# Moving work between steps of a two-recurrence pipeline: a 512-column split ahead of the candidate, routing one step earlier, two products into another PSUM bank

## What is computed

```
# LSTM, one step of 128
a = x_t @ Wx + h @ Wh + b;  i, f, o = sigmoid(...);  g = tanh(...)
c = f * c + i * g;  h = o * tanh(c)
# attention over the latents of h, then x = x + attn @ Wout
# GRU on the new x, one step of 128
z, r = sigmoid([x_t, h] @ Wz + bz), sigmoid([x_t, h] @ Wr + br)
cand = tanh([x_t, r * h] @ Wh + bh);  h = (1 - z) * h + z * cand
h_next = tanh(h @ Wp + bp) on every fourth step
# experts on the GRU's outputs: gate, top 2 of 8, gelu(x @ w1 + b1) @ w2 + b2, weighted sum, + x
```

## Time and profile before

| | |
|---|---|
| median of the runs | 589.99 us |
| the profiled execution | 591.56 us, its span 589.7 us |
| PE, DVE, ACT busy | 525.5, 424.1, 352.9 us |
| steps 74 to 81, one period of 8 | 31.01 us |
| PE busy in that period | 28.76 us |
| mean granted TensorE clock | 0.93 of 2.4 GHz |

### The profile page before, as it was taken

How to read it: one execution, slowest core, us unless ns; L and a number is a source line. 1 busy time by engine, 2 the same in 40 slices (tenths; PEclk the granted TensorE clock), 3 DMA queues, 4 the chain that set the end, 5 groups by cost and what they waited for, 6 DMA issues and landing times.

```text
span 589.7 us, 20148 instructions
## 1 busy us (share of the span) xinstructions
PE 525.5 (89%) x7315; PEld 483.4 (82%) x7356; DVE 424.1 (72%) x2402; ACT 352.9 (60%) x1297; POOL 33.6 (6%) x85
## 2 busy tenths in 40 slices
PE   7967887889789898989999989898999998889998
PEld 3736675888679898989888989898989988879998
DVE  4447678767776887878787878787879788664432
ACT  2235345775256676757676767676676767565562
POOL 6000000000000000000000000000000000000000
PEclk9679659699759999999999999999999999999999
DMA  8810101010100101010101010101101010100000
GB/s 204 327 15 6 20 1 20 3 13 10 16 11 6 16 5 17 12 20 3 19 12 17 7 15 16 12 10 12 16 14 13 4 17 13 18 1 3 11 7 10
DMA packets 75118, 14.32 MB, mean 24 GB/s; under 512 B 71411, under 2 KB 74111, under 8 KB 74638
## 3 DMA queue, kind: packets, MB, share of 16 engines
q1 hardware_dynamic: 74566, 11.96, 11.2%
q10 hardware_dynamic: 456, 1.08, 0.6%
HBM read 7.78 MB, written 1.05 MB: 15 GB/s over the span
## 4 chain that ended last, share of the span: by engine, by line
PE 68%; DVE 17%; issue 6%; ACT 6%; DMA 1%; SPq 1%; POOL 0%; DVEq 0%; ACTq 0%; POOLq 0%
PE pH L488 16%; PE pG L488 12%; PE pV L488 12%; PE pY L488 9%; PE pL L488 8%; PE pC L578 5%; PE pS L488 5%; ACT hid L864 2%; PE pC L488 2%; DVE latNlo L976 2%; DVE acc L1073 1%; DVE gB L1137 1%; DVE ghi L1140 1%; DVE glo L1143 1%; ACT gC L879 1%
## 5 line engine op out<-in xcount | busy, mean ns | idle before, releaser
L864 ACT ACTIVATE hid<-pH,b 128x256 f32<-128x256 f32 (+1 forms) x320 | 116.3, 433 | 3.9 <-PE pH L488 3.9
L488 PE MATMUL pY<-w,hid 128*128 128x128 f32 x608 | 85.1, 284 | 0.0
L488 PE MATMUL pH<-ghi,w1hi 128*128 128x256 f16 (+1 forms) x320 | 76.7, 254 | 9.1 <-ACT hid L864 7.3
L488 PE MATMUL pH<-ghi,w1lo 128*128 128x256 f16 (+1 forms) x320 | 77.0, 255 | 0.0
L488 PE MATMUL pH<-glo,w1hi 128*128 128x256 f16 (+1 forms) x320 | 76.9, 255 | 0.0
L488 PEld LDWEIGHTS pY<-w,hid 128*128 128x128 f32 x608 | 74.6, 193 | 0.2
L871 ACT ACTIVATE gT<-pG 128x32 f32<-128x32 f32 x128 | 24.7, 193 | 70.5 <-PE pG L488 70.3
L488 PE MATMUL pV<-w,hid 128*128 128x128 f32 x416 | 58.2, 283 | 0.0
L1124 DVE SCALAR_TENSOR_TENSOR gRZ<-gT,g 128x32 f32<-128x32 f32 x128 | 24.5, 191 | 46.6 <-ACT gT L871 46.0
L1137 DVE TENSOR_TENSOR gB<-gRZ,gC 128x16 f32<-128x16 f32 x128 | 22.5, 175 | 46.9 <-ACT gC L879 44.5
L879 ACT ACTIVATE gC<-pG 128x16 f32<-128x16 f32 x128 | 23.5, 183 | 52.9 <-PE pG L488 52.8
(11 more groups left out here) (177 smaller groups left out, 1569.6 us busy)
## 6 DMA issues: line engine op xcount, KB each, us to landing
w<-in_w SPq DMA_DIRECT2D x2, 2048.0 KB, 13.1
qbd<-qh SPq DMA_DIRECT2D x256, 16.0 KB, 1.9
out<-acc SPq DMA_DIRECT2D x16, 64.0 KB, 1.5
xT<-in_xT ACTq DMA_DIRECT2D x1, 960.0 KB, 8.2
hid<-in_WqT SPq DMA_DIRECT2D x1, 512.0 KB, 5.6
hid<-in_Wout SPq DMA_DIRECT2D x1, 512.0 KB, 10.3
lWh<-in_lWh SPq DMA_DIRECT2D x1, 256.0 KB, 2.8
lWx<-in_lWx SPq DMA_DIRECT2D x1, 256.0 KB, 3.1
```

Source lines behind the costliest of these rows:

```text
L488: return nc.tensor.matmul(o, lhsT=lhsT, rhs=rhs, start=start, stop=stop, skip_group_check=True)
L864: A(hid[:, e % NHID, c, 0:W], pH[half][:, W * at:W * (at + 1)], ACT.Gelu, bias=b1[:, e, c:c + 1], scale=1.0 / SP).then_inc(gelu, 1)
```

## The change

It reorders the loops and changes few operations.

- PTlo moves on DVE (k >= 18) from behind the cell to ahead of the wait for gC. mx moves ahead of slot B's combine. The cell is one block (rs now behind it), and latT and the rest of qh move from the start of the step into `between`, behind OT.
- Routing: `route_x` moves to the end of phase 1, its copies go to ACT at the end of that step (lg with a factor 0.5), route_first to phase 2; the subtraction `low` goes away, since tanh takes the negated maximum as its bias. latNhi and latNlo move to phases 2 and 3.
- Slot A of phases 2 and 3 goes to bank pC. Slot B's product of phase 6 goes to phase 0 (in pY).
- On ACT (k >= 18) the setup splits stand behind gT; the exp table is loaded behind gT of phase 3 and no more at the end of phase 2. The rest of qh is one DVE instruction in place of four.

```diff
-             (37, "B", 3, 0), (38, "B", 3, 1), (42, "A", 4, 0), ...
-             (44, "A", 6, 0), (44, "B", 6, 1), (45, "B", 7, 0), (46, "B", 7, 1))
+             (37, "B", 3, 0), (40, "B", 3, 1), (42, "A", 4, 0), ...
+             (44, "A", 6, 0), (44, "B", 6, 1), (45, "B", 7, 0), (48, "B", 7, 1))
 def route_stages(i):
-    at = GS * i + (26 if i < NG - 1 else 25)
-    if i > 12:
-        return at, at + 1, at + 2, at + 3, at + 3
-    return at, at + 1, at + 2, at + 6, at + 8
+    at = GS * i + 25
+    return (at, at + 1, at + 2, at + 3, at + 3) if i > 12 else (at, at + 1, at + 3, at + 7, at + 9)
+def down_bank(k, slot):
+    return "Y" if slot == "B" else "C" if k % TB in (2, 3) and k < LAST else "V"
-TO_EXP = [TB + O_S] + [k + 1 for k, half in UPS if half == 0 and (k + 1, 0) not in UPS and k < T]
+TO_EXP = [TB + O_S] + [k + 2 for k, half in UPS if half == 0 and (k + 1, 0) not in UPS and k < T]
 # turn_probs, then experts_down, on PE
+                if downs_before(k, "C"):
+                    pe.wait_ge(acc_done, downs_before(k, "C"))
+                        elif bank == "C":
+                            pe.wait_ge(q_lo, count(latents_at, k))
 # ACT, behind gT of the step
+                if k >= LAG:
+                    setup(k)
+                if k in TO_EXP:
+                    A(spare[:, 1:2], still[:, 0:1], ACT.Exp)
 # ACT, at the end of the step
-                setup(k)
+                if k < LAG:
+                    setup(k)
-                    A(th[:, n % 2, :], low[:, n % 2, :], ACT.Tanh, scale=0.5).then_inc(r_th, 1)
+                    A(th[:, n % 2, :], lg[:, n % 2, :], ACT.Tanh, bias=lmax[:, n % 2, 0:1]).then_inc(r_th, 1)
+                if k in ROUTES:
+                    route_copy(ROUTES[k])
 # DVE, between(k)
-                if unit_at(k, O_T) is not None:
+                if unit_at(k, O_T) is not None and k < LAG:
                     pt_rest(unit_at(k, O_T))
...
+                if latents_at(k) is not None:
+                    lat_copy(latents_at(k))
+                if latents_at(k - 1) is not None:
+                    q_rest(latents_at(k - 1))
...
-                if k % TB == 1 and TB < k <= T + 1:
+                if k % TB == 2 and TB < k <= T + 2:
                     turn_latents(k // TB - 1, lathi, latNhi)
 # DVE, the loop
+                if unit_at(k - 1, O_S) is not None:
+                    maximum(unit_at(k - 1, O_S))
                 if (k - 1, "B") in DOWN_AT:
                     combine(k - 1, "B")
+                if unit_at(k, O_T) is not None and k >= LAG:
+                    pt_rest(unit_at(k, O_T))
                 if k in PICK:
                     route_pick(PICK[k])
```

More of the change, by code:

```diff
@@ L117, in gelus_of, with downs_before @@
     return max(n for (vm, ve, h), n in GELUS.items() if (vm, ve) == (m, e))
-def downs_before(k, slot):
-    return max([ORDER[d] + 1 for (at, sl), ds in DOWN_AT.items() if sl == slot and at < k for d in ds], default=0)
+def downs_before(k, bank):
+    return max([ORDER[d] + 1 for (at, slot), ds in DOWN_AT.items() if down_bank(at, slot) == bank and at < k for d in ds], default=0)
 def count(at, upto):
@@ L374, in seq, with bank_of @@
             return t[:, :].rearrange("p (t b) -> p t b", b=B)[:, TB * p:TB * (p + 1), :].rearrange("p t b -> p b t")
-        def bank_of(slot):
-            return pV if slot == "A" else pY
+        def bank_of(k, slot):
+            return {"Y": pY, "C": pC, "V": pV}[down_bank(k, slot)]
         def keys(p):
@@ L405, in spread_queries @@
                 if u == 0:
[L406 removed]
+                    sp.wait_ge(q_lo, p + 1)
                 if n == 0:
@@ L829, in setup, with route_copy @@
                     A(gp, h0T[:, :], ACT.Copy).then_inc(g_p, 1)
+            def route_copy(n):
+                m, tg = visit_of(n)
+                act.wait_ge(r_mm, n + 1)
+                if n >= 2:
+                    act.wait_ge(r_ranked, n - 1)
+                A(lg[:, n % 2, :], pV[:, 256:256 + E], ACT.Copy, scale=0.5).then_inc(r_copy, 1)
+                if slots_used(m, tg):
+                    act.wait_ge(stored[2 * (m % 3) + tg], 16 * slots_used(m, tg))
+                A(acc[:, m % 3, tg, :], pV[:, 384:512], ACT.Copy).then_inc(r_copy, 1)
             def q_copy(p):
@@ L964, in q_rest @@
                 dve.wait_ge(q_hi, p + 1)
[L965 to L968, removed]
+                V.scalar_tensor_tensor(qh[:, p % 2, :, 1, :, :],
+                                       pC[:, :].rearrange("p (g s b) -> p b g s", g=HG, b=B), 1.0 / SP,
+                                       qh[:, p % 2, :, 0, :, :], ALU.mult, ALU.subtract).then_inc(q_lo, 1)
             def turn_latents(p, whole_t, turned):
@@ L1107, in setup_late, with cell, hidden @@
                     V.scalar_tensor_tensor(w1lo[:, e, :], w1[:, e, :], SW, w1hi[:, e, :], ALU.mult, ALU.subtract).then_inc(set_w1, 1)
-            def after_latents(k):
-                setup_late(k)
-                if latents_at(k) is not None:
-                    lat_copy(latents_at(k))
-                if latents_at(k - 1) is not None:
-                    q_rest(latents_at(k - 1))
-                if period_at(k) is not None:
-                    add_x(period_at(k))
+            def cell(t):
+                dve.wait_ge(l_tanh, t + 1)
+                V.scalar_tensor_tensor(lP[:, :, :], lT[:, 0:2, :], 1.0, lT[:, 3:5, :], ALU.add, ALU.mult).then_inc(l_mul, 1)
+                V.tensor_scalar(oK[:, :], lT[:, 2, :], SH / 2, SH / 2, ALU.mult, ALU.add)
+                dve.wait_ge(l_mul, t + 1)
+                V.scalar_tensor_tensor(lT[:, 4, :], lP[:, 1, :], 0.5, lP[:, 0, :], ALU.mult, ALU.add).then_inc(l_c, 1)
+            def hidden(t):
+                dve.wait_ge(l_tc, t + 1)
+                V.tensor_tensor(hhi[:, t + 1, :], oK[:, :], lC[:, :], ALU.mult).then_inc(l_hi, 1)
+                V.tensor_tensor(hfull[:, :], oK[:, :], lC[:, :], ALU.mult).then_inc(l_h, 1)
+                dve.wait_ge(l_h, t + 1)
+                V.tensor_tensor(hlo[:, t + 1, :], hfull[:, :], hhi[:, t + 1, :], ALU.subtract).then_inc(l_lo, 1)
             for k in range(STEPS):
@@ L1126, in _ @@
                     V.scalar_tensor_tensor(gA[:, :], gT[:, 1, :], -1.0, prev, ALU.add, ALU.mult).then_inc(g_a, 1)
+                if unit_at(k - 1, O_S) is not None:
+                    maximum(unit_at(k - 1, O_S))
+                if t < LAG:
+                    cell(t)
                 if (k - 1, "B") in DOWN_AT:
                     combine(k - 1, "B")
+                if period_at(k) is not None:
+                    add_x(period_at(k))
                 if k >= LAG:
-                    after_latents(k)
-                if unit_at(k - 1, O_S) is not None:
-                    maximum(unit_at(k - 1, O_S))
+                    setup_late(k)
+                if unit_at(k, O_T) is not None and k >= LAG:
+                    pt_rest(unit_at(k, O_T))
                 if k in PICK:
```

80 lines of the change are left out of this document (27 added, 53 removed).

## The result

The changed kernel takes 621.87 us (median of 4 runs, 621.58 to 623.97) against 590.0 (588.25 to 590.3): ratio 1.0554, 95% interval 1.0523 to 1.0585. The forecast was slower, 611 us, range 586 to 632. The profiled execution has a span of 620.0 us, 30.3 more than before.

What follows compares the result with a forecast made beforehand. PE was taken as near its limit, with DVE late in phases 2 to 5. Phase terms summed to +1.9, taken as +2.0 per period; ten periods plus outside steps gave +21, so 611 us, range 586 to 632.

Steps and rivals of the forecast that it cites:

- Phase 6, +0.55: Step 78: early PTlo delays gB, lC, table load and next gT; the product leaving gains nothing; +0.55 us per period.
- Phase 7, +0.05: Step 79: PTlo waits for PThi and holds gB, yet the state reaches PE in time; +0.05 us per period.
- Phase 0, +2.5: Step 80: moved product 1.0, PE's wait for latT 1.25, late start 0.76; +2.5 us per period.
- Phase 1, +0.3: Step 81: PE gets route_x, and the queries' spreading DMAs still end about when PE reaches the scores; +0.3 us per period.
- Phases 2 to 5, -1.5: Steps 74 to 77: PE loses route_x and waits for DVE, part given back; -1.5 us per period, bounds 0 and -2.0.
- steps 126 to 137: After the steady part: same order without the LSTM, latT wait still in step 128; +2 us.
- the first period, steps 46 to 53: First of the ten repeated periods, each forecast to lengthen by +2.0 us.
- my -1: Steps 18 to 33: gain from splits behind gT and a shorter DVE list; -1 us, bounds -4 and +3.
- The clock's rival: Poorly filled phases 7 and 0 drop PE's clock for three steps each period, another 2.4; 635 us, chance 0.15.
- The rival of a half hidden wait: Phase 0: latT comes in time for the moved product, 1.3 us less per period; 598 us, chance 0.10.
- the faster one: Phase 7 isn't held and phase 6 gives its 1.0 back, -1 to -2 per period; 574 us, chance 0.18.
- the rival of the Trainium skill: Phase 3: table switch costs load plus equally long drain, about 2.66 us; gC 1.1 later, ten times; no chance given.

Runs made afterwards that it cites:

- e2: Changed kernel with slot B's second-layer product back in phase 6, PTlo still early; 598.04 us, ratio 1.0131 to the kernel before.
- e10: Kernel before with only slot B's product moved from phase 6 to phase 0; 599.13 us, ratio 1.0149.
- e3: Changed kernel with latT and the rest of qh back at the start of their steps; 600.6 us, ratio 1.0166 to the kernel before.
- e6: Changed kernel with only the rest of qh back at the start of phase 1, latT still behind OT; 619.42 us, ratio 1.049 to the kernel before.
- e5: Changed kernel with PTlo behind the cell only where PThi is late (phase 7 with first-layer work); 616.22 us, ratio 1.0432 to the kernel before.
- e4: Changed kernel with PTlo behind the cell, the product in phase 6, latT and rest of qh early; 586.88 us, ratio 0.9936 to the kernel before.
- e7: e4 with PTlo ahead of gC in phases 4 and 5 only; 583.18 us, ratio 0.987 to the kernel before.
- e12: e7 with both latent transposes (latNhi and latNlo) in phase 1; 571.41 us, ratio 0.9677 to the kernel before.
- e9: e7 with latNhi moved to phase 1, latNlo left in phase 3; 576.57 us, ratio 0.9761 to the kernel before.
- e11: Kernel before with only PTlo moved ahead of the wait for gC; 598.04 us, ratio 1.0124.
- e1: Changed kernel with PTlo back behind the cell in every step; 612.79 us, ratio 1.0394 to the kernel before.
- e8: e7 with the latent transposes back in phases 1 and 2; 579.36 us, ratio 0.9805 to the kernel before.

## Why the prediction was right, and where its size was off

Slower was right, and the range held the time. The medians are 32 us apart, the profiled spans 30.3, the forecast was +21. By its own steps, with the means over steps 54 to 125 of before and of the changed kernel:

- Phase 6, +0.55: measured +0.42. gB 0.5 later, lC 0.47 later, the load at 2.97: the chain runs as written. That the product that left phase 6 gives nothing is shown by e2 against the changed kernel and by e10 against before.
- Phase 7, +0.05: 0.00 in the median, 0.18 in the mean, which is step 111 at the low clock. PE waited 1.05 us for gRZ, I had 1.4. The hold of gB is there, 1.44 us.
- Phase 0, +2.5: measured +2.62. PE waited 1.36 for latT (I had 1.25), hlo ended at 0.87 (0.8), the product started at 4.46 after gT (4.2). e3 and e6 price the wait for latT at 1.5 in a period, e5 the late start at 0.82.
- Phase 1, +0.3: measured +0.29.
- **Phases 2 to 5, -1.5: measured -0.37** (15.64 to 15.27). This term was mis-sized, and it is the miss: 1.13 us in each of nine periods, 10.2 us, while the other phases together come out as forecast. Two things are in it. First, I wrote that the spreading DMAs "still end at about the time at which PE reaches the scores". They end 0.1 us late in five of the nine periods and 1.2 to 1.6 late in the other four; e6, which removes just that, brings the four phases to 14.91, 0.4 less. Second, without it the gain is still only 0.7: DVE leaves PE waiting. I had counted DVE's list of phase 2 once, for gRZ of phase 3, and not its way on into phases 4 and 5; e4 shows DVE nearly full in phases 3 and 5, the early PTlo then shortens phase 5 (e7), and moving DVE's transposes away shortens phase 3 (e12). In e6's period of steps 74 to 77 PE idles for 0.92 us, where I had 0.5.
- Steps outside the steady part: steps 126 to 137 +4.0 (I had +2), with a stretch at 1.2 GHz in them; the first period, steps 46 to 53, is 0.6 shorter, where I had +2.0.
- Before step 46 the changed kernel is 0.8 ahead, near my -1, and that is luck. I had the gain in steps 18 to 33; these are 2.3 us longer (65.2 against 63.0) and steps 34 to 45 1.0 longer. What is won is won ahead of the first gT (59.6 us against 63.7), where ACT waits 2.38 us for pG in place of 5.11. The kernel before runs at 1.2 GHz for 3.4 us right there; how much of it is the change isn't shown.

One sum of the prediction is off: three steps at 0.9 us each are 2.7 in a period and not 2.4, so the clock's rival should have stood at 638 us, still the slowest case. The rival of a half hidden wait falls, since latT came after PE, and so does the faster one: its sign was a table load in phase 6 no later than 2.5 us after gT, and it came at 2.97.

The clock's rival came true in part: after 180 us the clock falls twice for 3.4 us in the changed kernel (at 449 and 521 us), in the kernel before never until the last 3 us. Step 111 was 1.6 us longer for it (5.37 against the median of 3.76), but step 112 behind it was 0.8 shorter (5.62 against 6.44), so this fall cost 0.8 us in all. It is not what makes the kernel slow, since the median steps, which it doesn't touch, carry the sum.

The table load behind gT of phase 3 delayed nothing in five of the nine periods, where gRZ comes about 1.2 after gT, as forecast. In the other four, those with the long phase 2, gRZ is in time (0.23 to 0.33 after gT) and the load is what gC waits for; the forecast had 0.5 for that case. The timeline of step 83, ACT and PE:

```profile
329.86 1.28 ACT L890 ACT_TABLE_LOAD   x1
330.47 0.29 PE L488 MATMUL pG<-gRZ,gW 128*128 128x16 f32 x2
331.27 0.17 ACT L898 ACTIVATE gC<-pG 128x16 f32<-128x16 f32 x1
```

gC starts 0.51 us after the candidate product ends; in step 75 it starts 0.04 after it. In e9 and e12, where DVE is early in phase 3, the 0.51 is there in every one of the nine periods; what it costs the step wasn't tested. The load follows gT at once (329.86 after 329.65), and behind its end at 331.14 come spare at 331.16 and gC at 331.27, with the next activations close behind. So a switch costs 1.28 us and the first activation, and no drain as long again shows; the rival of the Trainium skill (ScalarE: Activation LUTs, "What ACT_TABLE_LOAD costs"), 11 us more, falls.

Open: why the early PTlo of e11 gives 0.07 in phase 5 where it gives 0.46 in e7. It wasn't tried further.

## What to carry to other kernels

Look for the chain that ends a step, not for the engine that is full: in phase 6 PE was busy for all of 3.91 us and yet a product of 1.1 us could leave or come without changing the step, since a table load behind the last activation of the other recurrence set it (e10). An instruction belongs ahead of a critical wait only where its own producer is already done there and where nothing tight hangs behind the delay that it makes itself. The same edit shows all three cases: in phase 5 the early PTlo gained 0.46 us (e7), in phase 7 it waited for PThi and lost 0.82 a step later (e5), and in phase 6 its own time pushed the table load back and lost 0.46 (e1). When a wait is taken out of the full engine and the time doesn't fall, read the busy shares of the neighbouring steps: here DVE was next. From e4, 0.6% below the kernel before, PTlo early in phases 4 and 5 gave 1.3% (e7), and moving DVE's two transposes into the one step with room gave 3.2% (e12).

## What the runs showed of the hardware

The issue of a DMA on SP took 0.61 us in the median and 1.83 once in a window of ten, in the changed kernel between 323.4 and 330.5 us. Of the 160 issues that write qbd in steps 46 to 125, 13 took over 0.8 us. Three of the four periods with the long wait have one as their second issue, and step 90 has one as its fifth; the kernel before has such issues too, 10 of 160, but they come early enough to cost nothing. Between 323 and 330 us the profile shows one transfer of the instruction queue:

```profile
q8 instruction: 1, 0.02, 1.2%
```

The two go together: a transfer of this queue starts 1.3 to 1.9 us before the end of each of the 13 long issues, and of only 2 of the 147 short ones. No experiment changed it, so that it is the cause is not shown. Where nothing is left between the last landing and the scores, as here, one such issue is a wait of PE.

The granted clock fell to 1.2 GHz for short stretches in parts that the kernel before runs at 2.4 GHz throughout. Where the changed kernel falls, the two steps ahead have the work of every period, at the full clock (windows of steps 109 to 111):

```profile
440.16:444.22 4.06, 3.80 (x60) 3.62 (x59) 3.82 (x23) 2.44 (x11) 0.00 (x0) 1.00 0.05 6
444.22:448.64 4.42, 3.78 (x64) 3.26 (x62) 3.62 (x19) 3.67 (x11) 0.00 (x0) 1.00 0.07 19
448.64:454.01 5.37, 4.91 (x49) 4.31 (x50) 2.81 (x16) 2.73 (x10) 0.00 (x0) 0.68 0.00 0
```

The same work at the same places left the clock at 1.00 in step 79, so what decides between two periods stays open. Between kernels the falls go with the place of one product. All six profiles with the second-layer product in phase 0 have at least one stretch at 1.2 GHz between 180 us and the last 3 us of the span (the changed kernel, e1, e3, e5, e6, e10); none of the eight with it in phase 6 has one (before, e2, e4, e7, e8, e9, e11, e12). e2 and e10 differ from their kernels by that move alone. There is one profile of each, and by what path the move does it isn't shown.
